# DLRM interaction tower on one core: table look-ups for 512 samples at a time, and the last two tiles' layers taken one tile at a time

## The reference

```python
e = jnp.stack([tbl_0[ids[:, 0]], ..., tbl_26[ids[:, 26]]], axis=1)   # 2048 x 27 x 128
dot_products = jnp.einsum('bnd,bmd->bnm', e, e)
z = dot_products[:, c, r]            # the 351 pairs below the diagonal
h = jnp.concatenate([z, dense_ctx], axis=1)          # 2048 x 367
h = jnp.maximum(h @ W_top1 + b_top1, 0.0)            # 512 columns
h = jnp.maximum(h @ W_top2 + b_top2, 0.0)            # 256 columns
y = h @ W_top3
```

## Time and profile before

| | |
|---|---|
| time, median of 3 runs (lowest, highest) | 500.15 us (499.14 to 500.92) |
| span of the profiled execution, first to last instruction | 358.7 us |
| PE busy, share of the span | 333.7 us, 93% |
| POOL busy | 250.4 us, 70% |
| DVE busy | 246.3 us, 69% |
| ACT busy | 144.4 us, 40% |

### The profile page before, as it was taken

How to read it: one execution, slowest core, us unless ns; L and a number is a source line. 1 busy time by engine, 2 the same in 40 slices (tenths; PEclk the granted TensorE clock), 3 DMA queues, 4 the chain that set the end, 5 groups by cost and what they waited for, 6 DMA issues and landing times.

```text
span 358.7 us, 13616 instructions
## 1 busy us (share of the span) xinstructions
PE 333.7 (93%) x6094; PEld 303.4 (85%) x6094; DVE 246.3 (69%) x329; ACT 144.4 (40%) x265; POOL 250.4 (70%) x271
## 2 busy tenths in 40 slices
PE   1879699989999989999999999999999999999896
PEld 0779499978999979898889989999899989997775
DVE  3959979975488935878197965968387955961142
ACT  2536524444433433335343453435343353435320
POOL 5777777777777777777777777777777777777200
PEclk9969989999999999999999999999999999999999
DMA  6997744534333353443333452434533443322100
GB/s 184 306 318 196 205 136 107 102 93 91 83 93 82 90 99 75 96 96 80 93 88 82 115 85 77 105 84 81 102 89 83 99 98 74 84 55 55 27 3 1
DMA packets 26155, 36.86 MB, mean 103 GB/s; under 512 B 8451, under 2 KB 20099, under 8 KB 26098
## 3 DMA queue, kind: packets, MB, share of 16 engines
q0 software_dynamic: 8448, 17.32, 20.5%
q1 hardware_dynamic: 17506, 18.16, 20.1%
q10 hardware_dynamic: 144, 0.52, 0.4%
HBM read 35.97 MB, written 0.01 MB: 100 GB/s over the span
## 4 chain that ended last, share of the span: by engine, by line
PE 57%; POOL 26%; issue 10%; DVE 3%; DMA 3%; ACT 1%; DVEq 0%; ACTq 0%
POOL rows L450 26%; PE e_banks L482 25%; PE w_banks L543 9%; PE g_banks L513 8%; PE w_banks L554 7%; PE e_banks L494 6%; DMA rows<-in_tbl,idx 2%; DVE one_hot L672 2%; PE w_banks L532 1%; DVE zt L686 1%; DMA idx<-in_idx 1%; ACT et L340 0%; ACT h L333 0%; ACT et L350 0%; DVE a L720 0%
## 5 line engine op out<-in xcount | busy, mean ns | idle before, releaser
L450 POOL DMA_INDIRECT rows<-in_tbl,idx x264 | 249.6, 945 | 82.9 <-issue 78.0
L672 DVE TENSOR_TENSOR one_hot<-ids_wide,row_no 128x1024 fp32r<-128x1024 int32 x160 | 186.3, 1215 | 76.5 <-PE e_banks L482 72.5
L482 PE MATMUL e_banks<-one_hot,table_hi 128*128 128x256 f32 x672 | 172.2, 294 | 3.4 <-issue 3.4
L482 PE MATMUL e_banks<-one_hot,table_lo 128*128 128x256 f32 x672 | 167.0, 287 | 0.0
L482 PEld LDWEIGHTS e_banks<-one_hot,table_hi 128*128 128x128 f32 x672 | 131.4, 196 | 4.4 <-issue 4.2
L482 PEld LDWEIGHTS e_banks<-one_hot,table_lo 128*128 128x128 f32 x672 | 131.6, 196 | 0.2
L350 ACT ACTIVATE et<-e_banks 128x256 f32<-128x256 f32 x84 | 57.9, 689 | 89.3 <-PE e_banks L482 89.3
L340 ACT ACTIVATE et<-e_banks 128x512 f32<-128x512 f32 (+1 forms) x68 | 45.0, 664 | 52.3 <-PE e_banks L494 51.5
L513 PEld LDWEIGHTS g_banks<-et 128*26 128x26 f32 x4096 | 41.7, 103 | 17.7 <-issue 13.3
L513 PE MATMUL g_banks<-et 128*26 128x26 f32 x4096 | 50.0, 191 | 1.8 <-DVE zt L686 1.3
L494 PE MATMUL e_banks<-ident,rows 128*128 128x128 f32 x264 | 43.0, 285 | 5.5 <-DMA rows<-in_tbl,idx 5.5
(11 more groups left out here) (25 smaller groups left out, 67.7 us busy)
## 6 DMA issues: line engine op xcount, KB each, us to landing
ids_wide<-in_ids SPq DMA_DIRECT2D x80, 128.0 KB
et<-in_kept_tables SPq DMA_DIRECT2D x10, 512.0 KB, 10.1
rows<-in_tbl,idx POOLq DMA_INDIRECT x264
et<-in_kept_tables ACTq DMA_DIRECT2D x1, 512.0 KB, 3.9
a1T<-in_ids SPq DMA_DIRECT2D x4, 128.0 KB, 10.8
w<-in_w SPq DMA_DIRECT2D x2, 256.0 KB
w<-in_W_top SPq DMA_DIRECT2D x1, 512.0 KB
w<-in_w SPq DMA_DIRECT2D x1, 222.0 KB
```

Source lines behind the costliest of these rows:

```text
L450: pool.indirect_dma_start(rows[:, k % RING, a, :], None, tables[f], bass.IndirectOffsetOnAxis(ap=idx[:, t, f:f + 1], axis=0)).then_inc(row ...
L482: last = nc.tensor.matmul(e_bank[n % E_BANKS][:, 0:UNIT], part[:, q, c, :], one_hot[:, hot_slot(o, piece), c % PIECE, :], start=(c == 0 an ...
L672: nc.vector.tensor_tensor(one_hot[:, hot_slot(o, piece), :, :], ids_place(o).unsqueeze(1).broadcast_to([P, PIECE, UNIT]), row_no[:, piece ...
```

## The change

- **Look-ups for 512 samples.** In units 1 to 6 some look-ups (`WIDE_IN`: 3 features in unit 1, 5 in each of units 2 to 6) are made for the unit and the one after it at once: 16 matmuls of 512 columns, with a one-hot matrix in four pieces of two table chunks by 512 samples (each again 128x1024). ACT copies the first half into `et`, as before, and the second into a new buffer `halves`; later, when the next unit's place in `et` is free, ACT copies it there (step `place`). There are 28 wide and 29 narrow look-ups.
- **Unit 4 no longer gathers a look-up feature**, so there are 262 gathers and 66 chunks, against 264 and 68.
- **Rings.** `RING` 7 to 5 chunks, `IDS_RING` 4 to 3 places (each twice as long). The identity is kept once, in `ident_r`.
- **The end.** The pair products of tile 14 are done two ticks earlier. Tiles 14 and 15 take H and layer 1 one tile at a time (`H1`, `M1`: half the columns), tile 14 ahead of the last chunk's transposes or just behind them. Layer 2 of unit 6 also moves ahead of the last transposes. Of the layers, only tile 15's H1, M1 and L2 are left behind the last pack.

```diff
-GATHERED_IN = {0: 3, 4: 1}
+GATHERED_IN = {0: 3}
+WIDE_IN = {1: 3, 2: 5, 3: 5, 4: 5, 5: 5, 6: 5}
 PIECE = 4
-RING = 7
+RING = 5
-IDS_RING = 4
+IDS_RING = 3
...
+    wide, asked, over = {}, {}, []
+    for u in range(UNITS):
+        asked[u] = [q for q in looked_up(u) if q not in over]
+        wide[u] = over = asked[u][:WIDE_IN.get(u, 0)]
...
     for t in range(LAST_TILE):
         at = TILE_AT[t + 1] + (t == 0)
+        per_tick = 4 if t == LAST_TILE - 1 else 2
...
+    at, tile = TILE_AT[LAST_TILE], LAST_TILE - 1
+    turns[at] += [[("H", LAST - 1, c)] for c in range(KC)]
+    layers[at + 1] += [[("L1", LAST - 1, m)] for m in range(M1)]
+    layers[at + 2] += [[("L2", LAST - 1, j)] for j in range(PAIR)] + [[("H1", tile, c)] for c in range(KC)]
+    layers[at + 2] += [[("M1", tile, m)] for m in range(M1 // 2)]
+    layers[at + 3] += [[("M1", tile, m)] for m in range(M1 // 2, M1)]
...
+    END = pieces[:G_PIECES // 2] + [("L2", LAST, 0)] + pieces[G_PIECES // 2:] \
+        + [("turn", LAST_TILE), ("pack", LAST_TILE)] \
+        + [("H1", LAST_TILE, c) for c in range(KC)] + [("M1", LAST_TILE, m) for m in range(M1)] \
+        + [("L2", LAST, PAIR - 1)]
...
+            if (u, q) in WIDE:
+                j = wide[u].index(q)
+                if (u - 1, j) in PLACED:
+                    act.wait_ge(half_placed, PLACED[u - 1, j] + 1)
+                last = nc.scalar.activation(halves[:, j, :], e_bank[n % E_BANKS][:, UNIT:2 * UNIT], ACT.Copy)
+            last.then_inc(e_drained[n % E_BANKS], 1)
...
+        def place_half(act, s):
+            _, u, j = s
+            n = E_AT["OH", u, wide[u][j]]
+            act.wait_ge(g_filled, PAIR * u)
+            act.wait_ge(e_drained[n % E_BANKS], e_fills(n + 1, n % E_BANKS))
+            nc.scalar.activation(looked_up_et(u + 1, wide[u][j]), halves[:, j, :], ACT.Copy).then_inc(half_placed, 1)
```

More of the change, by code:

```diff
@@ L112, in dlrm_tower, with units_of @@
     TILE_AT = [CHUNK_AT[t, 0] for t in range(TILES)] + [TICKS]
-    LOOK_UPS = [(u, q) for u in range(UNITS) for q in looked_up(u)]
-    LOOK_UP_NO = {look_up: o for o, look_up in enumerate(LOOK_UPS)}
+    wide, asked, over = {}, {}, []
+    for u in range(UNITS):
+        asked[u] = [q for q in looked_up(u) if q not in over]
+        wide[u] = over = asked[u][:WIDE_IN.get(u, 0)]
+    WIDE = [(u, q) for u in range(UNITS) for q in wide[u]]
+    HALVES = max(len(wide[u]) for u in range(UNITS))
+    assert not wide[LAST] and all(q in looked_up(u + 1) for u, q in WIDE)
+    def units_of(look_up):
+        return 2 if look_up in WIDE else 1
     FIRST_LOOK_UPS = len(looked_up(0))
+    assert not wide[0]
     look_ups = [[] for _ in range(TICKS)]
@@ L156, in dlrm_tower @@
+    layers[at + 2] += [[("L2", LAST - 1, j)] for j in range(PAIR)] + [[("H1", tile, c)] for c in range(KC)]
+    layers[at + 2] += [[("M1", tile, m)] for m in range(M1 // 2)]
+    layers[at + 3] += [[("M1", tile, m)] for m in range(M1 // 2, M1)]
+    COLUMNS = {"T": 1024, "G": 768, "H": 768, "L1": 3072, "L2": 4096, "H1": 256, "M1": 1536}
+    LOOK_UP_COLUMNS = {1: 4608, 2: 8192}
     LOOK_UPS_FROM = [0, TILE_AT[1] + 1] + [TILE_AT[PAIR * (u - 1)] + 4 for u in range(2, UNITS + 1)]
-    load = [sum(COLUMNS[step[0][0]] for step in turns[k] + layers[k] + grams[k]) for k in range(TICKS)]
+    load = [COLUMNS["T"] + sum(COLUMNS[step[0][0]] for step in turns[k] + layers[k] + grams[k]) for k in range(TICKS)]
@@ L158, in dlrm_tower @@
     for u in range(1, UNITS):
         ticks = range(*LOOK_UPS_FROM[u:u + 2])
-        for q in looked_up(u):
+        taken = []
+        for q in asked[u]:
             k = min(ticks, key=lambda k: (load[k], k))
-            load[k] += COLUMNS["OH"]
-            look_ups[k].append([])
-        places = [(k, i) for k in ticks for i in range(len(look_ups[k]))]
-        for (k, i), q in zip(places, looked_up(u), strict=True):
-            look_ups[k][i] = [("OH", u, q)]
+            load[k] += LOOK_UP_COLUMNS[units_of((u, q))]
+            taken.append((k, units_of((u, q))))
@@ new lines, in dlrm_tower @@
+        taken.sort()
+        by_width = {n: iter([q for q in asked[u] if units_of((u, q)) == n]) for n in (1, 2)}
+        order = [(k, next(by_width[n])) for k, n in taken]
+        place_at = [(k, q) for k, q in order if q in wide[u]] or order
+        place_before = {q: j for j, (_, q) in enumerate(place_at) if j < len(wide[u - 1])}
+        assert len(place_before) == len(wide[u - 1])
+        for k, q in order:
+            before = [("place", u - 1, place_before[q])] if q in place_before else []
+            look_ups[k].append(before + [("OH", u, q)])
@@ L168, in dlrm_tower @@
     pieces = [("G", LAST_TILE, p) for p in range(G_PIECES)]
-    END = pieces[:G_PIECES // 2] + [("L2", LAST - 1, 0)] + pieces[G_PIECES // 2:] \
-        + [("turn", LAST_TILE), ("pack", LAST_TILE), ("L2", LAST - 1, 1)] \
-        + [("H", LAST, c) for c in range(KC)] + [("L1", LAST, m) for m in range(M1)] \
-        + [("L2", LAST, j) for j in range(PAIR)]
+    END = pieces[:G_PIECES // 2] + [("L2", LAST, 0)] + pieces[G_PIECES // 2:] \
+        + [("turn", LAST_TILE), ("pack", LAST_TILE)] \
+        + [("H1", LAST_TILE, c) for c in range(KC)] + [("M1", LAST_TILE, m) for m in range(M1)] \
+        + [("L2", LAST, PAIR - 1)]
@@ L473, in look_up @@
                     pe.wait_ge(lo_ready, o + 1)
-                elif u == 1 and q == looked_up(u)[0]:
+                elif o == FIRST_LOOK_UPS:
                     pe.wait_ge(hi_ready, NOH)
@@ L493, in transposes @@
                 for a in range(len(PLACES[t, i])):
-                    last = nc.tensor.transpose(e_bank[n % E_BANKS][:, a * P:(a + 1) * P], rows[:, k % RING, a, :], ident[:])
+                    last = nc.tensor.transpose(e_bank[n % E_BANKS][:, a * P:(a + 1) * P], rows[:, k % RING, a, :], ident)
                 last.then_inc(t_filled, 1)
@@ L733, in _ @@
             for q in range(LEAD):
-                make_one_hot(q)
+                for v in range(PIECE_AT[q], PIECE_AT[q + 1]):
+                    make_one_hot(v)
                 keep_rest(q)
```

182 lines of the change are left out of this document (123 added, 59 removed).

## The result

The change takes 487.64 us (median of 4 runs, 486.88 to 490.34) where the kernel before takes 500.45 (499.14 to 500.92) on the same chip: a ratio of 0.9756, 95% interval 0.9724 to 0.9788.

What follows compares the result with a forecast made beforehand. POOL's gathers and a PE some 2% slower were taken to run side by side; counted from T 15.1 at 323.6, the span ends at 354.3, plus 141.42 gives 495.7 us, range 493.9 to 499.4.

Steps and rivals of the forecast that it cites:

- the sum's frame: Whole run: the first profile's execution equals the median 500.15 us, so 141.42 us is added to the forecast span.
- it has in truth no free time: POOL from 4 to 334 us: gathers follow without a break, 1.250 us each, although POOL is shown busy only 70%.
- a lag of PE behind the rows: PE's transposes run behind POOL's gathers: 6.8 us at T 3.0, 11.8 at T 7.0, 10.4 at T 13.0, always under 13.
- starts with its rows: At T 15.1, two chunks before the last, PE has caught up and starts 2.1 us after the gathers, at 323.6 us.
- the 4.4 us counted from there on: From T 15.1 to the end: the span ends at 354.3 us, 4.4 us earlier than before.
- POOL waits on PE by more than 0.3 us: Sign that the forecast is wrong: POOL's gathers held back by PE, where at most 0.3 us was seen.
- the ring at nothing: Ring of 5 row places: holds POOL only at a PE lag near 20 us, so it costs nothing.
- The tail behind tile 15's products: From the end of tile 15's products to the end: 9.96 us, where it took 15.16 before.
- D: Rival: PE reaches T 15.1 late through dearer wide matmuls and short stalls, 1 to 3 us, 496.7 to 498.7; chance 0.12.
- B: Rival: the one-hot ring runs dry at wide look-ups, PE waits for DVE's pieces, slower, 505.4 at 0.5 us each; chance 0.10.
- A: Rival: PE's clock halves after waits for rows, costing 1.7 to 3.4 us in the tail, 497.4 to 499.1; chance 0.22.
- C: Rival: layer 1 for one tile costs as much as for two, 0.217 us an instruction, 500.8, no change; chance 0.06.

Runs made afterwards that it cites:

- 4: The kernel before with the change's two rings (rows 5 places, wide ids 3): 501.1 us, 0.9884; with the rows' ring alone: 494.7 us, 0.9836.
- 5: The change with the end of the kernel before (tiles 14 and 15 packed and layered together, unit 6's layer 2 in the tail): 492.2 us, 0.970.
- 2: The kernel before without unit 4's look-up gathers: 508.1 us, 0.9981; the change with those gathers put back: 498.3 us, 0.9829.
- 3: The change with narrow look-ups alone, no wide ones: 498.8 us, 0.9803.
- 10: The change with POOL's gathers also waiting for the first of two groups of products: 474.6 us, 0.934; the same with the old end: 473.0 us, 0.9324.
- 6: The change with 2 gathers for a chunk instead of 4, PE's instructions unchanged: 359.5 us, 0.709; with 3 gathers: 409.2 us, 0.8067.
- 7: The change with 2 gathers for a chunk and two POOL memsets in place of the other two: 368.9 us, 0.7343.
- second profile of before: The kernel before, unchanged, profiled again: 507.3 us, span 505.5 us.
- 11: The change with 3 places for gathered rows instead of 5: 483.9 us, 0.9604; the same with a later start of gathers and the old end: 458.8 us, 0.915.
- 9: The change with every other pair product left out, all gathers in place: 439.3 us, 0.8659.

## Why the prediction was wrong

**The step that failed** is the one that made the sum's frame: "That profiled execution is set equal to the median", with 141.42 us put around the span and carried over unchanged. That 358.7 us of span stood for an execution of 500 was not a constant but the sign that the profile was of another kind of execution. The page of the change had 1.8 us around its span. Everything that rests on POOL's pace fell with it: "it has in truth no free time", a lag of PE behind the rows, T 15.1 that "starts with its rows", and the 4.4 us counted from there on. The prediction's own sign of error came: "POOL waits on PE by more than 0.3 us", 123.0 us in all. The 4.4 us forecast for the end did not come either: from T 13.0 on the new end takes 88.1 us and the old one 88.0. That the direction came out right is luck; the gain lies where the prediction had counted none.

**Where the gain came from.** Between the two long profiles (505.5 and 486.3 us, from series that stand 1.4% apart with the kernel before, so the parts are too large in sum): to T 1.0 -8.8, from there to T 3.0 -1.2, from T 3.0 to T 13.0 -12.1, from T 13.0 to the end +2.9. The runs of one series show two parts. The rings take before from 507.3 to 501.1 us (4): they win at the start and lose 3 us behind T 13.0. Fewer gathers and wide look-ups together, with the old end, take it on to 492.2 (5), in the profiles all of it between T 3.0 and T 13.0 (290.7 to 281.8 us). How these 8.9 us are shared by the two is not shown; the ratios of other series put some 0.7% on the gathers (2) and 0.5% on the look-ups (3). The new end gives nothing (5, 10). The prediction priced **the ring at nothing**: "The ring of 5 holds it when PE is later with a chunk than POOL with the five after", at a lag near 20 us, and "The lags below stay under 13". It is held nearly always, and being held early is what shortens the start. Of the look-ups it said "The gain is not what PE's busy time loses", since rows would set the pace; with POOL waiting for PE, that reason was gone.

**What held, by its own rows.** A wide matmul: 0.23 taken, 0.23 measured (365.17 to 365.40). By the formula of the Trainium skill ("TensorE: Matmul & The Clock Gate", "Back-to-back issue gap"), which the page gives for a single matmul by itself, it would be 0.216 us; the trace of the change is against it. M1's instruction: 0.11 taken; 12 of them lie between 468.60 and 470.04, 0.12 each. The tail behind tile 15's products: 9.96 worked out, 11.7 measured against 15.3 in the kernel before; most of the difference is M1 of tile 15, which took 4.4 us (477.23 to 481.63) where 2.8 were counted. It did not wait for its banks: its 24 instructions follow each other without a break, 0.11 us apart up to 478.1 and then 0.21, because the granted clock stood at its lower level (0.50) from 478.13 to 481.55, after 2.4 us in which PE had been busy 0.89. These two stretches as windows (the clock is the third number from the end):

```profile
474.80:477.20 2.40, 0.89 (x4) 0.45 (x3) 1.84 (x7) 0.96 (x4) 0.00 (x0) 1.00 0.00 0
477.20:481.60 4.40, 4.40 (x25) 4.38 (x25) 0.35 (x1) 1.01 (x3) 0.00 (x0) 0.61 0.01 4
```

From T 15.1 to the end 30.7 worked out, 31.9 measured. The arithmetic of the end was sound; it shortened a stretch that began at the rows in the one profile and begins behind PE's own work in the timed runs.

**The rivals.** D, PE late at T 15.1, is what happened, for a reason of its own. B did not: DVE's pieces were not waited for in units 2 to 6. A: the clock did fall (mean 0.937 in the change, 0.895 in the second profile of before), behind standstills rather than for rows. One fall lay in the tail, behind PE's wait for the last pack, and cost M1 1.7 us, the lower of A's two prices; two more signs of error came with it, the clock at 0.5 after 300 us and M1's instructions 0.2 apart. C, by the 0.12 above at the full clock, did not.

**Shown and not shown.** Shown: gathers, far more than POOL's work, make the products stand (6, 7); the tick follows their number (6); a shorter first run of gathers shortens the start (4, 11). Open: what in a gather holds the other engines back, and why one execution of the kernel before had hardly any of it (13.3 us inside the products) with the same gathers at the same pace of 1.250 us. Late blocks of instructions can't be it for most of the standstills: the trace of the change lists 45 blocks of 16 KB on an instruction queue against 113 standstills of over 0.4 us inside the products, and only 3 of these end within 0.35 us of a block's end. In half the products (9) POOL itself paused 1.3 us between chunks whose place was free, which the lock-step does not explain.

## What to carry to other kernels

Set the span beside the time first: where they differ by a quarter, the profile is of another execution, and a forecast from it holds for that execution alone; ask for a second profile before a sum is made. Where one engine issues indirect DMAs all the time, look at the idle time inside runs of small matmuls with no releaser, and vary the number of gathers: if the tick follows, place the gathers under long instructions, try a shorter lead and count what it costs behind the last rows as well as what it wins at the start, and try a start of the gathers when the run of small ones is nearly over.
